# A two-network graph attention kernel on one core: the second turned head of each slot is copied out of PSUM by VectorE, not by ScalarE

## What is computed

```python
for l in range(3):                                # the first network
    scores = leaky_relu(si[:, :, None] + sj[:, None, :] + attn_b[l], 0.2)
    attn = softmax(where(mask, scores, -inf))
    h = layernorm(x + attn @ x, g1[l], beta1[l])
    ff = gelu(h @ W1[l] + b1[l]) @ W2[l] + b2[l]
    x = layernorm(h + ff, g2[l], beta2[l])
x = _layernorm(x_in + x)
xh = (x @ W_proj).reshape(B, N, H, k).transpose(0, 2, 1, 3)    # the second network, H = 8, k = 32
att = softmax(where(A > 0, leaky_relu(a_src[..., None] + a_dst[..., None, :] + b_att), NEG_INF))
x = _layernorm(x + relu(att @ xh))
```

## Time and profile before

| | us |
|---|---|
| median of 3 runs | 2459.54 |
| lowest and highest | 2458.81, 2459.89 |
| the profiled execution | 2460.2 |
| its span, first to last instruction | 2458.4 |

### The profile page before, as it was taken

How to read it: one execution, slowest core, us unless ns; L and a number is a source line. 1 busy time by engine, 2 the same in 40 slices (tenths; PEclk the granted TensorE clock), 3 DMA queues, 4 the chain that set the end, 5 groups by cost and what they waited for, 6 DMA issues and landing times.

```text
span 2458.4 us, 33996 instructions
## 1 busy us (share of the span) xinstructions
PE 2317.6 (94%) x11361; PEld 1647.6 (67%) x11361; DVE 1669.2 (68%) x5647; ACT 1779.6 (72%) x3415; POOL 171.4 (7%) x200
## 2 busy tenths in 40 slices
PE   2999999999999999999999999999999999999775
PEld 1676766767766766776677677767766776677543
DVE  6445875587656877668666777568765686666477
ACT  1434477777878768787687877787787877888685
POOL 0000100000000000000000001000000000000000
PEclk9999999999999999999999999999999999999967
DMA  5111121012111031011120120210220111200010
GB/s 182 35 35 35 54 71 57 22 65 87 43 53 48 31 104 60 22 50 65 64 69 23 65 82 27 74 48 31 97 67 18 52 36 60 65 18 22 31 44 31
DMA packets 85785, 131.59 MB, mean 54 GB/s; under 512 B 4424, under 2 KB 53868, under 8 KB 85612
## 3 DMA queue, kind: packets, MB, share of 16 engines
q1 hardware_dynamic: 85612, 129.41, 16.1%
HBM read 120.74 MB, written 8.65 MB: 53 GB/s over the span
## 4 chain that ended last, share of the span: by engine, by line
PE 79%; ACT 11%; DVE 7%; issue 1%; DMA 1%; POOL 0%; SPq 0%; DVEq 0%; POOLq 0%; ACTq 0%
PE ffn L1130 21%; PE ffn L1117 12%; PE av L1117 12%; PE av L1053 12%; PE pT L1036 11%; PE av L1069 4%; ACT prob L451 3%; PE av L1156 3%; ACT prob L445 2%; DVE prob L702 2%; PE av L1104 2%; ACT xs L485 1%; PE trow L1017 1%; ACT prob L438 1%; PE ffn L1128 1%
## 5 line engine op out<-in xcount | busy, mean ns | idle before, releaser
L1130 PE MATMUL ffn<-w_sb,G 128*128 128x256 f32 x3072 | 745.0, 380 | 0.0
L1130 PEld LDWEIGHTS ffn<-w_sb,G 128*128 128x128 f32 x3072 | 551.0, 190 | 73.9 <-issue 13.2
L702 DVE CUSTOM_DVE_ANT_0 prob<-trow,mask 128x512 f32<-128x512 f32 x704 | 457.5, 686 | 184.9 <-PE trow L1017 147.9
L1036 PEld LDWEIGHTS pT<-ident,prob 128*128 128x128 f32 x2816 | 356.6, 145 | 211.0 <-issue 130.9
L1036 PE MATMUL pT<-ident,prob 128*128 128x128 f32 x2816 | 440.9, 282 | 49.3 <-DVE prob L747 18.9
L451 ACT ACTIVATE prob<-prob,nm 128x512 f32<-128x512 f32 x512 | 362.6, 711 | 0.0
L1117 PE MATMUL ffn<-hT,w_sb 128*128 128x512 f32 x768 | 357.3, 595 | 1.1 <-ACT hT L464 1.1
L1117 PE MATMUL av<-hT,w_sb 128*128 128x512 f32 x768 | 356.1, 593 | 0.0
L445 ACT ACTIVATE prob<-prob,s 128x512 f32<-128x512 f32 x512 | 346.9, 713 | 11.3 <-DVE nm L709 11.3
L460 ACT COPY prob<-pT 128x512 f32<-128x512 f32 x452 | 259.4, 580 | 101.7 <-PE pT L1036 100.8
L401 POOL TENSOR_TENSOR rstd<-veps,mhalf 128x4 f32<-128x4 f32 x127 | 152.7, 1202 | 2242.5 <-DVE veps L637 2242.5
(11 more groups left out here) (113 smaller groups left out, 2502.5 us busy)
## 6 DMA issues: line engine op xcount, KB each, us to landing
w_sb<-in_L_gnn_W SPq DMA_DIRECT2D x48, 1024.0 KB, 7.4
trow<-rows_dram SPq DMA_DIRECT2D x128, 256.0 KB, 3.2
adj_sb<-in_adj SPq DMA_DIRECT2D x16, 1024.0 KB, 5.3
xin<-in_x SPq DMA_DIRECT2D x16, 512.0 KB, 6.3
x0r<-in_x SPq DMA_DIRECT2D x16, 512.0 KB, 4.5
out<-o SPq DMA_DIRECT2D x15, 512.0 KB, 3.3
aw_row<-in_L_gnn_attn_w SPq DMA_DIRECT2D x1, 768.0 KB
g_row<-in_L_gnn_g SPq DMA_DIRECT2D x2, 384.0 KB
```

Of the source, the lines that this page charges most:

```text
L702: return v.tensor_tensor_reduce(out=out_[:, t, :], in0=targets, in1=mask[:, t, :], scale=1.0, scalar=LEAST, op0=ALU.add, op1=ALU.max, accu ...
L1036: last = te.transpose(pT[bank][:, j * P:(j + 1) * P], src[:, t, j * P:(j + 1) * P], ident[:])
L1130: last = te.matmul(ffn[part][:, at:at + D], G[:, f, t * P:(t + 1) * P], w2_sb[:, g // 2 % STAGES, f, :], start=False, stop=f == FT - 1)
```

## The change

For the second head of `turned(g)`, in the slots 7 to 46, the four copies out of `pT` are taken from ScalarE's program and put into VectorE's, behind `attention` (with the maxima that close it) and ahead of `graph_out` and `fed_forward(s, 0)`. `by_dve` is true for these heads, so that TensorE signals VectorE (`pd`) and waits for VectorE's copies (`copy`). The second head of slot 47 stays with ScalarE, and so do the first and third heads of all slots. These are 40 heads, 160 copies. Line numbers behind the edit shift by one or two.

```diff
         def by_dve(q, t):
 
 
-            return q is not None and q >= LAST_HEADS - 1 and (t < T - 1 or q >= LAST_HEADS + HEADS - 1)
+            if q is not None and q < LAST_HEADS - 1:
+                return any(turned(g)[1:2] == [q] for g in range(UNITS - 1))
+            return q is not None and (t < T - 1 or q >= LAST_HEADS + HEADS - 1)
 
...
                 if place == 0:
                     head_rows(four)
-                for q in heads[1:2] if att else []:
-                    for t in range(T):
-                        turned_out(q, t)
                 if att:
                     normalise(ATTENDED, y_att, xs[s2], s_hn)
...
                     attention(s2, l2, *new[1:2])
+                for q in turned(g)[1:2] if att else []:
+                    for t in range(T):
+                        turned_out(q, t)
                 if done is not None:
                     graph_out()
```

## The result

The changed kernel takes 2555.47 us, the median of 4 runs (2554.16 to 2556.23), against 2459.18 us before (2458.53 to 2459.89, 4 runs): a ratio of 1.0391, interval 1.0373 to 1.0409, 96 us slower. The forecast was 2525.0 us, from 2508 to 2540. The profiled execution took 2555.8 us, with a span of 2554.0.

The account below looks back on a forecast made before the run. TensorE was taken to bound the slots. Stalls of 66.5 us over 40 slots, less 2 us returned by ScalarE, plus 1 us for restarts, gave 65.5 on 2460.2: 2525.7, against the median 2525.0 us; range 2508 to 2540.

Parts of the forecast that it names:

- The bound: In the slots TensorE bounds the time (matmuls busy 1271.57 of 1290 us), so every microsecond it is held comes out.
- The price of one slot: TensorE's third turned tile (tile 2) waits for VectorE's first copy: difference of starts + 0.84 us, 2.11 us in slot 21.
- that range: Copy price: 0.69 us taken; ScalarE's 0.59 us takes 3 us off the sum, slowed bank access puts 3 us on.
- No second stall: Behind tile 2, tile 3's bank is free and the third head's copy needs 1.5 us against 2.7 available.
- kind 2 free: In slots numbered 2 modulo 6, the copy is ready before TensorE wants the bank: no stall, 1.13 us to spare.
- VectorE's lateness: After its copies VectorE falls 1.39 us back against TensorE; its later waits cover this, so it costs nothing.
- the wait for the target row after kind 4: Sign: after slots numbered 4 modulo 6, VectorE's wait for the target row shrinks by about 1.2 us, never gone.
- What ScalarE gets back: ScalarE loses 94 us of copies, mostly otherwise waiting; about 2 us return in slots 5 modulo 6, waits at slot starts unchanged.
- kind 1's wait: In slots numbered 1 modulo 6, TensorE's 0.40 us wait for ScalarE's late copy goes, leaving 1.56 us of stall.
- Rival 1: Stalls partly absorbed: a freed ScalarE gets ahead at slot starts, up to 23 us back, 2502 us; chance 0.05.
- Rivals 2, 4 and 5: 2: VectorE's lateness reaches target rows, 2545, 0.05; 4: TensorE works past tile 2, 2458, 0.03; 5: copies hide, 2433, 0.03.
- rival 3: Clock falls: 10 us at half clock after each of 33 stalls, some 5 us each, 165 us, 2690 us; chance 0.01.

Follow-up runs that it names:

- e1: Kernel before, second heads' copies left on ScalarE but held until VectorE made the next second head's maxima: 2552.5 us, ratio 1.0379.
- e6: Changed kernel with the change only for second heads in slots numbered 3, 4, 5 modulo 6, ScalarE keeping the rest: 2521.0 us, ratio 1.0248.
- e7: Changed kernel with the change only for second heads in slots numbered 0, 1, 2 modulo 6: 2487.0 us, ratio 1.0114.
- e8: Changed kernel with 16 transposes of the identity added on TensorE ahead of slot 0: 2550.1 us, ratio 1.0371.
- e9: Changed kernel with the four copies also behind fed_forward(s, 0), except in slots numbered 2 modulo 6: 2577.3 us, ratio 1.0480.
- e5: Changed kernel with VectorE's first copy behind the fourth target tile, the rest behind the maxima; slots 2 modulo 6 as changed: 2511.1 us, ratio 1.0213.
- e2: Changed kernel with VectorE's first copy behind the third target tile, second behind the fourth, rest behind the maxima; slots 2 modulo 6 as changed: 2488.7 us.
- e4: Changed kernel with VectorE's copies behind the last attended tile, the statistics, the third and the fourth target tile: 2452.3 us, ratio 0.9972.

## Why the forecast was wrong

- **The bound** was read rightly: TensorE's stalls came out at the end one for one, in every run.
- **The price of one slot** held to the rows' digit: 2.11 us in slot 21. In sum 65.2 us idle in 33 waits, longest 2.3; the forecast said 60 to 66, 33 times, longest 2.5. The copy's 0.69 us and the hand-over of 0.15 us held (1087.02 + 0.69 + 0.15 = 1087.86, and tile 2 starts at 1087.85), and the other end of that range, ScalarE's price, is what e1 shows: no cheaper in the sum.
- **No second stall** and **kind 2 free** held: no wait for a copy in front of tile 3, and none in slot 20.
- **VectorE's lateness** cost nothing, as worked out, but one sign did not come true: the wait for the target row after kind 4 was to be shorter by about 1.2 us, and after slot 22 it is still 1.20 us. What shrank is the wait in front of it, for the heads turned back: 0.80 us and not 1.36 in slot 22, and gone in slot 40, which has no fall; it took up VectorE's lateness. After slot 23 (kind 5) the row's wait is 4.98 us, where it was 5.90 (the earlier trace rows has the same of slot 11). With a fall TensorE itself is late, so in such slots the cover was not put to the full test.

```profile
1155.03 0.69 DVE L834 TENSOR_TENSOR o<-av,rec 128x512 f32<-128x512 f32 x1 [0.80 <-PE av L1079]
...
1167.60 0.69 DVE L701 CUSTOM_DVE_ANT_0 prob<-trow,mask 128x512 f32<-128x512 f32 x1 [1.20 <-PE trow L1019]
...
1219.61 0.69 DVE L701 CUSTOM_DVE_ANT_0 prob<-trow,mask 128x512 f32<-128x512 f32 x1 [4.98 <-PE trow L1019]
```

- **What ScalarE gets back** held in both parts: kind 1's wait is in the subtraction, kind 5 gives 0.27 us a slot where 0.3 was put, and the waits of TensorE on ScalarE at slot starts did not change (18.4 and 5.0 us again). Rival 1 had nothing. Rivals 2, 4 and 5 did not come about.
- **The step that failed is the clock.** The sum has no term for it: the clock stands only in rival 3, with a chance of 0.01 and a price of 165 us. The forecast and the rival were set against each other as alternatives, and what came was the forecast plus a fifth of the rival: 19 falls and not 33, 1.68 us each and not 5. The evidence against it was read too far. A wait of up to 1.7 us at clock 1.00 says nothing of 2.1 us, as the text itself noted, and that gap was then left out of the range. With 1.7 us bounding the cost from one side and the last part, where the clock does fall, from the other, the range had to reach from 2525 to 2525 plus 33 falls; by the 1.68 us now measured that is 2580, and it would have held 2555.

The Trainium skill, "TensorE: Matmul & The Clock Gate" (Part 1), was cited for the rule that inactivity lowers the clock. The trace agrees in the slots too: the clock is 0.50 behind 19 of the 33 stalls of 2.1 us, and stays at 1.00 behind those of 1.7 us.

Which stalls bring a fall is not the kind of the slot: over the profiled runs there are falls at 19, 19, 12, 3, 17 and 19 of 33, 33, 20, 13, 33 and 33 stalls of 2.1 us or more (changed kernel, e1, e6, e7, e8, e9), in sets that differ between kernels whose slots are alike, and at 0 of 66 of 1.1 and 1.7 us. The clock records of these runs show that it is the moment. Within one profile all falls begin on one even beat, to 0.01 us: the two shown under the result begin 51.2 us apart, and the others of that profile keep the same beat. In the changed kernel, e1, e6, e7 and e8 there are 132 stalls with 1.9 to 2.3 us of idle time. In 68 of them the idle time begins 0.1 to 1.4 us behind a point of the beat, and all 68 have a fall. Of the 64 others two have one (slot 9 in the changed kernel and in e8, idle for 2.18 us). That is why kinds 3, 4 and 5 had all 19 falls in the changed kernel: their tiles 2 come 51.3 us apart (531.32 and 582.61 in slots 10 and 11) and so meet the beat at the same place, and those of kinds 0 and 1 behind them meet it 1.6 us later. The length counts as well: six stalls of e5 and 15 of e2 begin at that same place and have no fall. This was read off after the runs; no kernel was built to forecast a set of falls from it.

The runs of one kernel spread by 12 us in e1, 9 in e6, 5 in e8, 4 in e9 and 2 in the changed kernel, and by 4, 3 and 1 us in e2, e4 and e5. That the number of falls differs from run to run would explain the wide ones, but only one run of each was profiled.

## What to carry to other kernels

Work that moves to an engine with idle time costs nothing only at the right place in that engine's order: find when the buffer is wanted back, and put the copy ahead of whatever on that engine can wait (here targets of a head that is needed a slot later), which is the difference between 96 us lost and 7 us won. The stall is a subtraction of two starts in the trace plus the copy and the hand-over, and holds to a few per cent. Where the bound engine is TensorE and the stall is longer than any that the trace shows at full clock, add the half-clock stretch that may follow to the upper end of the range (here each stall of 2.1 us was followed by one or not by its moment alone, so a forecast without that moment has to span both), and don't count a rival's cost as excluding the forecast's.

## What the runs showed of the hardware that was not expected

One idle time of some 1.9 to 2.3 us (by the row) in an otherwise unbroken stream of matmuls can be followed by, or overlap, some 3.4 us at granted clock 0.50, 1.68 us lost, nearly as much as the stall itself. It depends on when the idle time begins: the granted clock fell only at points of an even beat. After 1.5 to 1.9 us of idling a fall was never seen in 33 stalls. A 128 x 512 copy out of PSUM takes 0.69 us on VectorE and 0.59 us on ScalarE, and this difference of 0.1 us played no part in any of the results.
